# Edge convolution on one core: minimum trees two batches at a time over three tiles, and at most two chain steps in a row

## The chip, the cores and the metric

The kernel runs on one core of a Trainium2 chip. The core's engines work side by side and meet through semaphores: TensorE (PE in the profile, with its weight loads as PEld), VectorE (DVE), ScalarE (ACT), GpSimd (POOL) and SyncE (SP, which here only issues transfers). Each engine takes its instructions in the order in which the program holds them. The metric is the device time of one execution in microseconds (us), lower is better; the time of a kernel is the median of its runs.

## The reference

```python
def _L0_gnn_ref(x, W, b, edge_index):
    src, dst = (edge_index[0], edge_index[1])
    x_i = x[dst]
    x_j = x[src]
    feat = jnp.concatenate([x_i, x_j - x_i], axis=-1)
    msg = feat @ W.T + b
    out = jax.ops.segment_max(msg, dst, num_segments=x.shape[0])
    return jnp.where(jnp.isfinite(out), out, 0.0)
edge_index = jnp.stack([src, dst])
h = jnp.maximum(_layernorm(x, axis=-1), 0.0)
x = x + _L0_gnn_ref(h, L0_gnn_W, L0_gnn_b, edge_index)
```

There are 6250 nodes with 128 channels in float32 and 206250 edges (100000 random pairs in both directions, and a loop at every node), sorted by destination. The part of a message that belongs to the destination is the same for all its edges, so what has to be found is, for each destination and channel, the maximum over its sources j of one row `near[j]` = W2 h[j].

## The kernel before

Destinations lie on a grid of 128 partitions by 49 columns; sources are cut into 49 tiles of 128. After a first part (layer norm, products, and for each destination a sorted list of its sources) the maximum is taken in two ways at once.

**Dense part.** For each destination and each source tile t one edge, the winner, goes through TensorE. The minimum over |source - 256 t| along a destination's sorted list gives the winner's row in the tile. ScalarE makes these numbers (`distances(g)`, L616, one ACTIVATE for each of the two tiles of batch g), and VectorE takes the minimum by halving (`tree(g)`: L1326, L1331, then, once for each two batches, L1340 and L1345, which writes `M`). There are 25 batches. SP stores `M` to `winners` and loads it back broadcast over all partitions (784 KB for a tile, at most six tiles ahead); ScalarE turns it into a one-hot matrix (`one_hot(t)`, L621), and TensorE multiplies the tile's rows of `near` by it, in three bf16 parts, into PSUM: 39 matmuls of 481 columns for a tile, in four rounds of 12, 9, 9 and 9. After each round VectorE takes the maximum of PSUM and `acc` (`dense_round`, L1373). PSUM holds two rounds, so TensorE can start round n when VectorE is through with round n - 2.

**Chain.** Every edge that isn't a winner of its tile is a loser. Losers stand in a list of 504 steps (the last one is empty), a step holding one edge for each partition. For each step GpSimd gathers 128 rows of `near_table` (L765), four steps to a block; a block is issued when the block two before it has landed and when the chain has passed the slot that it overwrites, six blocks back. VectorE adds each step to a running maximum (`chain_step`, L1317). SP stores the running maxima eight steps at a time to `running_max` (L485), and a last gather, `finals` (L744, 49 of them, one for each column), takes for each destination the row at which its run ends. These finals overwrite the memory that the trees use, and the first of them waits until all trees are done. Nine groups of four are issued between gathers, after steps 432, 440, ... 496; the other 13 columns come behind the last gather, and the last two of these need the very last store. Then `join(g)` (L1430, L1432, 13 groups) takes the maximum of `acc` (transposed by TensorE) and these rows, adds the destination's own part, and SP stores the result in two or three transfers for each group (L517, L518, L521).

**What sets the order.** VectorE's program is one list of pieces, made by `schedule()`: the second list's sorting and compaction, then 49 tiles of four rounds, with tree pieces between them. Six trees stand ahead of the tiles (`EARLY_TREES`); before the change, one tree follows each of the tiles 0 to 18. The planner goes through the pieces with a cost for each and a model of the gathers, and puts up to `MOST_STEPS` chain steps behind a piece where their rows should have landed (`served`). Steps that find no place come after the tiles, mixed with the joins (`rest_steps`): 16 before the change. Of the other 488, all stand in runs of four: 25 runs ahead of the tiles, 97 in them. SP's order (stores, loads) follows the same list.

Of the kernel before, what the change touches and what calls it, by code (L numbers as in the profile page):

```python
# [45 lines left out]

CUTS = ((36, 400), (44, 472), (47, 496), (49, 504))
FINALS_FROM, FINALS_EVERY = 432, 8
LANDING, MARGIN, MOST_STEPS = 4.6, 1.5, 4
JOINS = 2  # L50
UNITS = ((0, 4), (4, 7), (7, 10), (10, 13))
PAD = 8190
# [9 lines left out]
def stages(h):  # L62
    a, z, _ = PARTS[h]
    return ((z - a) * KS + LEFT * h - 1).bit_length()


FLAG_PIECES, WORD_PIECES = 6, 5
EARLY_TREES = 6
TREES_FROM = 2


def window(g):

    per_tile, before, upto = 32.0 / 49, g // 2 * 4, min(g // 2 * 4 + 3, 48)
    low, high = per_tile * before, per_tile * upto
    first = max(0, math.floor(low - 2.75 * math.sqrt(low)))
    count = max(8, -(-(math.ceil(high + 2.75 * math.sqrt(high) + 2) - first) // 4) * 4)
    first = min(first, KM - count)
    return first, first + count


def last_halvings(g):

    first, end = window(g)
    n, left = (end - first) // 4, []
    while n > 2:
        n -= n // 2
        left.append(n)
    return left


def tree_pieces(g):

    first, end = window(g)
    half = (end - first) // 2 * 100
    costs = [0.17 + half * 0.00052, 0.17 + half * 0.00026]
    if g % 2 or g == 24:
        costs += [0.17 + n * 200 * 0.00052 for n in last_halvings(g)] + [0.4]
    return [("tree", c) for c in costs]


def schedule():

    pieces = [("lists", 11.0, 2.2), ("check", 1.1, 1.5), ("check", 1.9, 1.5), ("check", 1.9, 1.5)]
    pieces += [("sort", 1.42, 1.5)] * 21 + [("tiles", 2.3, 1.7)]
    pieces += [("flags", cost, 1.8) for cost in (2.05, 2.6, 2.5, 2.5, 1.4)]
    pieces += [("words", cost, 1.8) for cost in (3.5, 1.2, 1.2, 1.2, 3.0, 1.2, 3.0)]  # L110
    trees = 0
    for i in range(stages(1)):
        long = i < stages(1) - 3
        pieces += [("move", 1.5, 1.5)] + [("move", 0.8, 1.5)] * 4 if long else [("move", 0.8, 1.5), ("move", 1.3, 1.5)]
        if TREES_FROM <= i < TREES_FROM + EARLY_TREES:
            pieces += [(name, cost, 1.6) for name, cost in tree_pieces(trees)]
            trees += 1
    pieces += [("list", 2.2, 1.4), ("verdict", 0.2, 1.3)]
    pieces += [("disorder", 0.8, 1.3)]
    for t in range(49):  # L120
        for r in range(4):
            pieces += [("round", (2.15, 1.65, 1.65, 1.65)[r], 1.26)]
        if trees < 25:
            pieces += [(name, cost, 1.3) for name, cost in tree_pieces(trees)]
            trees += 1
    first, total = PARTS[0][2], PARTS[0][2] + PARTS[1][2]
    finals = {FINALS_FROM + g * FINALS_EVERY: GROUP for g in range(CUTS[0][0] // GROUP)}
    now, issue, n, landed, done, listed, steps = 0.0, 0.0, 0, [], [], None, []
    for name, cost, gather in pieces:
        now += cost  # L130
        if name == "list":
            listed = now
        here = []
        while n < total and len(here) < MOST_STEPS:
            if len(landed) <= n:
                b = n // GATHERS
                if n == first:
                    if listed is None:
                        break
                    issue = max(issue, listed)  # L140
                if b >= SLOTS:
                    issue = max(issue, done[(b - SLOTS + 1) * GATHERS - 1] + 0.2)
                if b >= FLYING:
                    issue = max(issue, landed[(b - FLYING) * GATHERS])
                issue += GATHERS * gather
                landed += [issue + LANDING] * GATHERS
                issue += 1.25 * finals.get((b + 1) * GATHERS, 0)
            if landed[n] + MARGIN > now:
                break
            now += 0.355  # L150
            done.append(now)
            here.append(n)
            n += 1
        steps.append(here)
    return [name for name, _, _ in pieces], steps, list(range(n, total)), first, total


def edgeconv(nc, x, src, dst, W, b, out):
# [10 lines left out]
    chk_p = 125  # L169
    chk_w = edges // chk_p  # L170
    CT = sum(c for _, _, c in PARTS)
    early_groups = CUTS[0][0] // GROUP
    spans = [(a, min(a + GROUP, tiles)) for a in range(0, tiles, GROUP)]
# [3 lines left out]
    batches = [(a, min(a + 2, tiles)) for a in range(0, tiles, 2)]  # L177
    rounds = len(UNITS)
    names, served, rest_steps, first_steps, all_steps = schedule()
    first_blocks, all_blocks = first_steps // STEPS, all_steps // STEPS  # L180
    assert D == P and tiles == 49 and rest and 0 < lastj and CUTS[-1] == (tiles, CT) and lastp == P - 1
# [15 lines left out]
    with ExitStack() as ctx:  # L197
# [337 lines left out]
        def _(act):  # L535
# [72 lines left out]
            def distances(g):  # L608
                if g == 0:
                    act.wait_ge(k2_ready, 2)  # L610
                if g >= 2:
                    act.wait_ge(y_free, g - 1)
                a, z = batches[g]
                first, end = window(g)
                for t in range(a, z):
                    nc.scalar.activation(y[g % 2][:, t - a, 0:end - first, :], k2[:, first:end, :], ACT.Abs,  # L616
                                         bias=off[:, t:t + 1]).then_inc(y_made, 1)

            def one_hot(t):
                act.wait_ge(bytes_in[t % OHS], 16 * (t // OHS + 1))  # L620
                nc.scalar.activation(oh[t % OHS], oh_bytes[t % OHS], ACT.Abs_reciprocal_sqrt, bias=spike[:, 0:1],  # L621
                                     scale=float(SPIKE), saturate=False).then_inc(oh_ready, 1)

            a, z, _ = PARTS[1]
            numbers, at = words[1][1], LEFT + (z - a) * KS
# [9 lines left out]

            for g in range(EARLY_TREES):
                distances(g)
            for t in range(tiles):
                one_hot(t)
                if t + EARLY_TREES < len(batches):  # L640
                    distances(t + EARLY_TREES)

        def edge_by_edge(pool):
            HALF = P // 2
# [65 lines left out]
        def _(pool):  # L710
# [24 lines left out]
            for h, (a, z, _) in enumerate(PARTS):  # L735
                pool.wait_ge(starts_ready, h + 1)
                for j in range(a + a % 2, z, 2):
                    nc.gpsimd.indirect_dma_start(L_pairs[:, j // 2, :], None, src_pad[:, None],  # L738
                                                 bass.IndirectOffsetOnAxis(start_i[:, j:j + 1], 0)).then_inc(list_in[h], 16)
# [43 lines left out]
            for (a, _), (z, cap) in zip(CUTS, CUTS[1:]):  # L783
                stored(cap // STEPS)
                finals(a, z)
# [670 lines left out]
```

## Time and profile before

| what | value |
|---|---|
| time, median of 3 runs | 839.28 us (838.05 to 840.8) |
| time of the profiled execution | 839.78 us |
| its span, first to last instruction | 838.1 us |
| mean granted TensorE clock | 0.881 of full speed |
| busy: VectorE, GpSimd, TensorE, ScalarE | 92%, 69%, 65%, 50% of the span |

The span is 1.7 us shorter than the time of the same execution, which holds some work around it. Busy shares are means over the whole span. GpSimd's gathers each show about 0.94 us of busy time and 0.3 us ahead of the next one, so an engine that issues gathers without a pause shows some 75% busy.

### The profile page before, as it was taken

To read this page: it belongs to the slowest core of one execution; us is meant where nothing else is said; L and a number is where in the kernel's file an instruction comes from. 1 tells how busy PE (TensorE), PEld (TensorE's weight loads), DVE (VectorE), ACT (ScalarE), POOL (GpSimd) and SP (SyncE) were. 2 spreads that over 40 slices of the span, in tenths; PEclk is the share of its full clock that TensorE was granted. 3 is DMA by queue.
4 is the path that set the end of the run, shared out by engine and by line. 5 is a ranking of instruction groups with operands and counts; after the bars stand their busy time and mean duration, and the time that the engine had idled before them with its cause. 6 is when DMAs were issued, how large, how long until landed. Compare 5 with 4: busy or idle time off the path is not lost.

```text
span 838.1 us, 7993 instructions
## 1 busy us (share of the span) xinstructions
PE 540.9 (65%) x2442; PEld 260.6 (31%) x2442; DVE 767.7 (92%) x1264; ACT 422.2 (50%) x279; POOL 579.0 (69%) x609
## 2 busy tenths in 40 slices
PE   1564898000006678676767667888888888888871
PEld 1553466000002233232322222333333333333340
DVE  8999999989997998899898999899999998888896
ACT  3876314520390756567565878555555556560000
POOL 1650477777777777677777777777777777777772
PEclk9999899555557998898988897999999999999995
DMA  8590023232647655555555555556555666642336
GB/s 251 148 254 26 16 69 98 69 101 79 201 101 226 173 174 144 167 167 155 176 146 163 153 180 155 177 186 193 180 178 173 187 179 181 218 129 77 103 101 197
DMA packets 114071, 126.77 MB, mean 151 GB/s; under 512 B 19176, under 2 KB 96470, under 8 KB 113885
## 3 DMA queue, kind: packets, MB, share of 16 engines
q1 hardware_dynamic: 95090, 86.33, 33.9%
q0 software_dynamic: 18752, 38.98, 17.7%
q10 hardware_dynamic: 186, 0.96, 0.3%
q8 instruction: 19, 0.31, 0.2%
q14 instruction: 24, 0.20, 0.1%
HBM read 86.46 MB, written 40.57 MB: 152 GB/s over the span
## 4 chain that ended last, share of the span: by engine, by line
DVE 35%; PE 18%; issue 15%; DVEq 0%
DVE acc L1373 20%; PE ps L888 18%; DVE maxima L1317 10%; DVE hT L1326 2%; DVE hT L1430 1%; DVE hT L1340 1%; DVE hT L1331 1%; DVEq L1372 0%; DVE M L1345 0%; DVE hT L1432 0%; PE ps L876 0%; DVEq L1313 0%; DVEq L913 0%; DVEq L1330 0%; DVE spare L1351 0%
## 5 line engine op out<-in xcount | busy, mean ns | idle before, releaser
L765 POOL DMA_INDIRECT rows<-near_table,idx x503 | 502.6, 999 | 202.1 <-issue 137.6
L1373 DVE TENSOR_TENSOR acc<-ps,acc 128x1924 f32<-128x1924 f32 x196 | 343.7, 1780 | 35.0 <-PE ps L888 34.6
L888 PE MATMUL ps<-ohs,near 128*128 128x481 fp8e3 x1404 | 320.4, 383 | 84.9 <-DVE acc L1373 76.6
L621 ACT ACTIVATE ohs<-ohs,spike 128x6272 fp8e3<-128x6272 uint8 x36 | 197.8, 5513 | 70.6 <-DMA ohs<-winners 70.6
L888 PEld LDWEIGHTS ps<-ohs,near 128*128 128x128 bf16 x1404 | 134.8, 101 | 270.5 <-DVE acc L1373 95.3
L1317 DVE SCALAR_TENSOR_TENSOR maxima<-maxima,fresh,rows 128x128 f32<-128x128 f32 x503 | 177.1, 352 | 13.6
L616 ACT ACTIVATE hT<-k,off 128x1600 bf16<-128x1600 int16 (+6 forms) x49 | 65.9, 1391 | 148.0 <-DVE hT L1331 148.0
L888 PE MATMUL ps<-sorts_mem,near 128*128 128x481 fp8e3 x507 | 114.9, 381 | 29.0 <-DVE acc L1373 26.9
L621 ACT ACTIVATE sorts_mem<-sorts_mem,spike 128x6272 fp8e3<-128x6272 uint8 x13 | 71.7, 5515 | 30.8 <-DMA sorts_mem<-winners 30.8
L888 PEld LDWEIGHTS ps<-sorts_mem,near 128*128 128x128 bf16 x507 | 48.8, 101 | 94.9 <-DVE acc L1373 31.7
L876 PE MATMUL ps<-flags,ones 128*128 128x14 f32 x2 | 0.6, 368 | 113.7 <-DVE spare L1351 113.7
L744 POOL DMA_INDIRECT hT<-running_max,end_row x49 | 47.4, 968 | 19.0 <-issue 14.0
L738 POOL DMA_INDIRECT ohs<-src_pad,start_i x25 | 25.0, 1000 | 19.3 <-DVE start_i L1002 12.3
L876 PEld LDWEIGHTS ps<-flags,ones 128*128 128x128 f32 x2 | 0.5, 310 | 113.9 <-issue 113.9
L1279 DVE COPY_PREDICATED ohs<-ohs 128x556 int32<-128x556 int32 (+9 forms) x40 | 29.7, 742 | 1.1
L603 ACT COPY base<-ps 128x512 f32<-128x512 f32 (+1 forms) x13 | 7.3, 561 | 40.7 <-PE ps L859 40.7
L859 PEld LDWEIGHTS ps<-wT,hT 128*128 128x128 f32 x98 | 23.5, 310 | 5.1 <-issue 3.7
L830 PE MATMUL ps<-wT,hT 128*128 128x128 f32 x98 | 13.9, 286 | 15.8 <-ACT near L588 15.8
L804 PE MATMUL ps<-ident,k 128*128 128x128 f32 x49 | 9.1, 311 | 22.6 <-ACT k L558 22.6
L859 PE MATMUL ps<-wT,hT 128*128 128x128 f32 x98 | 22.4, 373 | 0.0
L1326 DVE TENSOR_TENSOR hT<-hT 128x1600 bf16<-128x1600 bf16 (+7 forms) x25 | 20.6, 826 | 0.0
L558 ACT ACTIVATE k<-acc,shift,rstd 128x128 f32<-128x128 f32 x49 | 20.1, 482 | 0.6 <-DVE shift L983 0.6
(200 smaller groups left out, 425.3 us busy)
## 6 DMA issues: line engine op xcount, KB each, us to landing
running_max<-maxima SPq DMA_DIRECT2D x63, 512.0 KB, 3.6
ohs<-winners SPq DMA_DIRECT2D x36, 784.0 KB, 6.5
sorts_mem<-winners SPq DMA_DIRECT2D x13, 784.0 KB, 6.6
rows<-near_table,idx POOLq DMA_INDIRECT x503, 3.3
acc<-in_x SPq DMA_DIRECT2D x6, 512.0 KB, 6.1
near_table<-acc SPq DMA_DIRECT2D x12, 256.0 KB, 5.3
base<-in_x SPq DMA_DIRECT2D x1, 2744.0 KB
out_x<-hT SPq DMA_DIRECT2D x12, 224.0 KB
```

Source lines behind the costliest of these rows:

```text
L558: last = nc.scalar.activation(xn[:, g % 2, j - spans[g][0], :], x_nat[:, j, :], ACT.Identity, bias=shift[:, j:j + 1], scale=rstd[:, j:j + 1])
L616: nc.scalar.activation(y[g % 2][:, t - a, 0:end - first, :], k2[:, first:end, :], ACT.Abs, bias=off[:, t:t + 1]).then_inc(y_made, 1)
L621: nc.scalar.activation(oh[t % OHS], oh_bytes[t % OHS], ACT.Abs_reciprocal_sqrt, bias=spike[:, 0:1], scale=float(SPIKE), saturate=False).th ...
L738: nc.gpsimd.indirect_dma_start(L_pairs[:, j // 2, :], None, src_pad[:, None], bass.IndirectOffsetOnAxis(start_i[:, j:j + 1], 0)).then_inc( ...
L744: nc.gpsimd.indirect_dma_start(rowsF[:, j, :], None, running_max[0:cap * P, :], bass.IndirectOffsetOnAxis(end_row[:, j:j + 1], 0)).then_in ...
L765: nc.gpsimd.indirect_dma_start(rows[:, n % (SLOTS * GATHERS), :], None, near_table[:, :], bass.IndirectOffsetOnAxis(idx[:, n:n + 1], 0)).t ...
L859: last = nc.tensor.matmul(bank(g % 3)[:, (j - a) * D:(j - a + 1) * D], hT[:, j:j + (P - 1) * tiles + 1:tiles], wT[:, 1, :], start=False, s ...
L888: last = nc.tensor.matmul(bank(4 * (n % 2) + c - UNITS[r][0])[:, 0:CHUNK], near[:, t, part, :], oh[t % OHS][:, at:at + CHUNK], start=part ...
L1279: then(V.copy_predicated(word[:, u:v], moves[:, u:v], word[:, u + d:v + d]))
L1317: V.scalar_tensor_tensor(run_at(n + 1), run_at(n), fresh[:, n:n + 1], rows[:, n % (SLOTS * GATHERS), :], ALU.add, ALU.max).then_inc(chain, 1)
L1326: then(V.tensor_tensor(mine[:, 0:n, 0:half, :], mine[:, 0:n, 0:half, :], mine[:, 0:n, half:2 * half, :], ALU.min))
L1373: V.tensor_tensor(into, found[:, 0:z - a, 0:CHUNK], into, ALU.max).then_inc(max_done, 1)
```

## The change

The trees of two batches (four tiles) are now one group of pieces, spread over the twelve rounds of three tiles; the ten groups stand in tiles 2 to 31. ScalarE's distances for such a group come in one go, after the one-hot matrix of the tile before it. A run of chain steps has at most two steps. The planner's costs for rounds and steps are a little lower. The computation is the same. The number of trees, rounds, steps, gathers and transfers is the same.

```diff
-LANDING, MARGIN, MOST_STEPS = 4.6, 1.5, 4
+LANDING, MARGIN, MOST_STEPS = 4.6, 1.5, 2
+STEP, NEXT_STEP = 0.26, 0.38
...
+TREE_TILES, TREES_AT = 3, 2
...
+def pair_begins(k):
+    return TREES_AT + TREE_TILES * (k - EARLY_TREES // 2)
+
+
+def pair_pieces(k):
+    return [piece for g in range(2 * k, min(2 * k + 2, 25)) for piece in tree_pieces(g)]
...
-            pieces += [("round", (2.15, 1.65, 1.65, 1.65)[r], 1.26)]
-        if trees < 25:
-            pieces += [(name, cost, 1.3) for name, cost in tree_pieces(trees)]
-            trees += 1
+            pieces += [("round", (2.1, 1.6, 1.6, 1.6)[r], 1.26)]
+            k = (t - TREES_AT) // TREE_TILES + EARLY_TREES // 2
+            if t >= TREES_AT and k <= 12:
+                at, late = (t - pair_begins(k)) * 4 + r, pair_pieces(k)
+                pieces += [(name, cost, 1.3) for name, cost in late[at * len(late) // (4 * TREE_TILES):
+                                                                    (at + 1) * len(late) // (4 * TREE_TILES)]]
...
-            now += 0.355
+            now += NEXT_STEP if here else STEP
...
-                if t + EARLY_TREES < len(batches):
-                    distances(t + EARLY_TREES)
+                for k in range(EARLY_TREES // 2, -(-len(batches) // 2)):
+                    if t == pair_begins(k) - 1:
+                        for g in range(2 * k, min(2 * k + 2, len(batches))):
+                            distances(g)
```

On VectorE, tile 9 stood before as follows (`acc<-ps` is a round, `maxima` the chain steps, `hT` and `M` the tree):

```order
L1373 TENSOR_TENSOR acc<-ps,acc 128x1924
L1373 TENSOR_TENSOR acc<-ps,acc 128x1443
L1317 SCALAR_TENSOR_TENSOR maxima<-maxima,fresh,rows 128x128 x4
L1373 TENSOR_TENSOR acc<-ps,acc 128x1443 x2
L1317 SCALAR_TENSOR_TENSOR maxima<-maxima,fresh,rows 128x128 x4
L1326 TENSOR_TENSOR hT<-hT 128x2x800
L1331 TENSOR_TENSOR hT<-hT 128x2x400
L1340 TENSOR_TENSOR hT<-hT 128x4x200
L1340 TENSOR_TENSOR hT<-hT 128x4x100
L1317 SCALAR_TENSOR_TENSOR maxima<-maxima,fresh,rows 128x128 x4
L1345 SCALAR_TENSOR_TENSOR M<-hT 128x200
```

In the changed kernel, whose line numbers are 12 to 14 higher, tile 9 holds:

```order
L1387 TENSOR_TENSOR acc<-ps,acc 128x1924
L1387 TENSOR_TENSOR acc<-ps,acc 128x1443
L1331 SCALAR_TENSOR_TENSOR maxima<-maxima,fresh,rows 128x128 x2
L1340 TENSOR_TENSOR hT<-hT 128x2x700
L1331 SCALAR_TENSOR_TENSOR maxima<-maxima,fresh,rows 128x128 x2
L1387 TENSOR_TENSOR acc<-ps,acc 128x1443
L1331 SCALAR_TENSOR_TENSOR maxima<-maxima,fresh,rows 128x128 x2
L1345 TENSOR_TENSOR hT<-hT 128x2x350
L1331 SCALAR_TENSOR_TENSOR maxima<-maxima,fresh,rows 128x128 x2
L1387 TENSOR_TENSOR acc<-ps,acc 128x1443
```

The tree's pieces stand singly, with two steps on either side; before, thirteen instructions stood between the last round of this tile and the first of the next. The steps come to 96 in 48 runs ahead of the tiles, 376 in 188 runs in them, and 32 behind them.

Behind the last round, VectorE's program ended before with 15 steps and 13 joins (two rows each), which began:

```order
L1317 SCALAR_TENSOR_TENSOR maxima<-maxima,fresh,rows 128x128 x8
L1430 TENSOR_TENSOR hT<-ps,hT 128x512
L1432 TENSOR_TENSOR hT<-hT,base 128x512
L1430 TENSOR_TENSOR hT<-ps,hT 128x512
L1432 TENSOR_TENSOR hT<-hT,base 128x512
L1317 SCALAR_TENSOR_TENSOR maxima<-maxima,fresh,rows 128x128 x4
```

Nine joins then stood behind the last step. Now 31 steps follow the tiles, two joins after each four of them, and the program ends so (the first row is the last run of steps):

```order
L1331 SCALAR_TENSOR_TENSOR maxima<-maxima,fresh,rows 128x128 x7
L1444 TENSOR_TENSOR hT<-ps,hT 128x512
L1446 TENSOR_TENSOR hT<-hT,base 128x512
L1444 TENSOR_TENSOR hT<-ps,hT 128x512
L1446 TENSOR_TENSOR hT<-hT,base 128x512
L1444 TENSOR_TENSOR hT<-ps,hT 128x512
L1446 TENSOR_TENSOR hT<-hT,base 128x512
L1444 TENSOR_TENSOR hT<-ps,hT 128x128
L1446 TENSOR_TENSOR hT<-hT,base 128x128
```

Nine joins moved ahead of the last step, and four are left behind it. On SP the stores of eight groups' results moved ahead of the last store of running maxima, and five are left behind it. GpSimd's order is unchanged.

## Rows read from the trace of the kernel before

**Rows 1.** Timeline of GpSimd: start, us, instruction, [idle before it, and its releaser].
```profile
94.17 1.25 POOL L765 DMA_INDIRECT rows<-near_table,idx  x1 [38.16 <-DVE idx L1300]
...
805.01 0.94 POOL L765 DMA_INDIRECT rows<-near_table,idx  x1 [0.30 <-issue]
...
819.54 1.03 POOL L744 DMA_INDIRECT hT<-running_max,end_row  x1 [0.30 <-issue]
824.99 0.94 POOL L744 DMA_INDIRECT hT<-running_max,end_row  x1 [4.41 <-DMA running_max<-maxima]
826.23 0.94 POOL L744 DMA_INDIRECT hT<-running_max,end_row  x1 [0.31 <-issue]
```

**Rows 2.** Waits of the whole span, GpSimd's gathers: us in total, times, longest.
```profile
POOL rows L765 <- issue: 137.6, 443, 1.4
...
POOL rows L765 <- DMA rows<-near_table,idx: 17.1, 34, 3.4
...
POOL rows L765 <- DVE maxima L1317: 9.3, 25, 1.3
```

**Rows 3.** Waits of the whole span, VectorE's rounds and ScalarE's distances.
```profile
ACT hT L616 <- DVE hT L1331: 148.0, 21, 31.6
...
DVE acc L1373 <- PE ps L888: 34.6, 47, 3.9
```

**Rows 4.** Issue to landing of transfers from 780 us on, count, us.
```profile
hT<-running_max,end_row POOLq DMA_INDIRECT x19, 2.6
rows<-near_table,idx POOLq DMA_INDIRECT x15, 2.5
```

**Rows 5.** Timeline of VectorE behind the last round (809.88 us on).
```profile
809.88 3.12 DVE L1317 SCALAR_TENSOR_TENSOR maxima<-maxima,fresh,rows 128x128 f32<-128x128 f32 x8
812.92 0.68 DVE L1430 TENSOR_TENSOR hT<-ps,hT 128x512 f32<-128x512 f32 x1
...
820.71 0.68 DVE L1430 TENSOR_TENSOR hT<-ps,hT 128x512 f32<-128x512 f32 x1
...
831.32 0.28 DVE L1430 TENSOR_TENSOR hT<-ps,hT 128x128 f32<-128x128 f32 x1
831.64 0.29 DVE L1432 TENSOR_TENSOR hT<-hT,base 128x128 f32<-128x128 f32 x1
```

**Rows 6.** Timeline of SP's issues behind the last chain step.
```profile
820.82 0.36 SPq L485 DMA_DIRECT2D running_max<-maxima  x1
821.22 0.58 SPq L517 DMA_DIRECT2D out_x<-hT  x1
...
835.36 0.38 SPq L517 DMA_DIRECT2D out_x<-hT  x1
835.79 0.45 SPq L518 DMA_DIRECT2D out_x<-hT  x1
```

**Rows 7.** Timeline of VectorE in tiles without trees (638 to 653 us).
```profile
638.62 3.72 DVE L1373 TENSOR_TENSOR acc<-ps,acc 128x1924 f32<-128x1924 f32 x2
642.26 1.51 DVE L1317 SCALAR_TENSOR_TENSOR maxima<-maxima,fresh,rows 128x128 f32<-128x128 f32 x4
643.68 3.23 DVE L1373 TENSOR_TENSOR acc<-ps,acc 128x1443 f32<-128x1443 f32 x2
646.82 1.51 DVE L1317 SCALAR_TENSOR_TENSOR maxima<-maxima,fresh,rows 128x128 f32<-128x128 f32 x4
```

**Rows 8.** Timeline of VectorE, the last step of a run of four and what follows.
```profile
419.78 0.35 DVE L1317 SCALAR_TENSOR_TENSOR maxima<-maxima,fresh,rows 128x128 f32<-128x128 f32 x1
420.05 0.36 DVE L1345 SCALAR_TENSOR_TENSOR M<-hT 128x200 uint8<-128x200 bf16 x1
```

**Rows 9.** Busy us (and instructions) by engine in two stretches, granted clock, DMA share, GB/s.
```profile
420.40:515.70 95.30, 67.67 (x273) 27.67 (x273) 87.47 (x131) 69.82 (x20) 72.05 (x74) 0.86 0.58 161
...
613.00:700.00 87.00, 74.88 (x350) 32.72 (x351) 82.85 (x101) 48.30 (x10) 64.84 (x70) 1.00 0.64 197
```

**Rows 10.** Pieces of the chain that ended last, start, us: rounds on TensorE.
```profile
693.57 2.64 PE ps L888 x12
...
710.50 2.03 PE ps L888 x9
```

**Rows 11.** Costliest groups, ScalarE's one-hot matrices and distances: busy us, mean ns.
```profile
L621 ACT ACTIVATE ohs<-ohs,spike 128x6272 fp8e3<-128x6272 uint8 x36 | 197.8, 5513 | 70.6 <-DMA ohs<-winners 70.6
...
L616 ACT ACTIVATE hT<-k,off 128x1600 bf16<-128x1600 int16 (+6 forms) x49 | 65.9, 1391 | 148.0 <-DVE hT L1331 148.0
```

## The prediction, made before the changed kernel ran

> **What bounds the kernel now.** VectorE is busy for 92% of the span, so the eye goes there first. The stage that ends last says something else. I read GpSimd's timeline, then its waits, then the tail on VectorE and SP, and only then the rounds.
>
> GpSimd issues its first gather at 94.17 and its last one, step 502, at 805.01 [rows 1]. In these 710.8 us it issues 503 gathers and 32 of the finals. Each shows 0.94 us and 0.30 us ahead of the next, 1.25 us in all [rows 1], so 535 of them need at least 669 us. Its waits beyond that 0.30 are few: on landings 17.1 - 34 x 0.30 = 6.9 us, on the chain's slots 9.3 - 25 x 0.30 = 1.8 us, and under "issue" 137.6 - 443 x 0.30 = 4.7 us [rows 2]; the rest up to 711 us are gathers that take longer than 0.94 us, most of them ahead of the tiles. So GpSimd runs from 94 us to the end with 13.4 us of waiting in it. It is a second bound beside VectorE, and the change gives it no instruction less.
>
> VectorE ends its rounds at 809.88 [rows 5], 5 us behind the last gather's issue, still with 15 steps to do. Behind that the tail of before has a chain of its own. The last step leaves at 820.71 [rows 5]. SP stores the maxima at 820.82 [rows 6], and GpSimd, through with 11 finals at 819.54 + 1.03 = 820.57, waits 4.41 us for that store and issues the last two finals at 824.99 and 826.23 [rows 1]. Nine joins stand behind the last step, the last at 831.32 [rows 5], and SP issues all 13 results behind the last store, until 835.79 + 0.45 = 836.24 [rows 6]; the span ends 1.9 us later. SP's row of issues ends last here.
>
> **What the change does on VectorE.** Number of operations: equal. What it saves is the space between chain steps. A run of four takes 643.68 - 642.26 = 1.42 us until the next instruction [rows 7]; the last step of a run hands over after 420.05 - 419.78 = 0.27 us [rows 8], so a step that the next step waits for costs (1.42 - 0.27)/3 = 0.38 us. A run of two then costs 0.38 + 0.27 = 0.65 us, an estimate, since none stands in the trace. Ahead of the tiles: 25 x 1.42 = 35.5 before, 48 x 0.65 = 31.2 now, 4.3 less. In the tiles: 97 x 1.42 = 137.7 before, 188 x 0.65 = 122.2 now, 15.5 less. So with nothing else the rounds end at 809.9 - 19.8 = 790.1.
>
> Here the Trainium skill speaks against the change: "VectorE: DVE Perf Modes", section "The DRAIN you can't avoid", says that the next instruction doesn't start until the pipeline is empty and that chaining operations without semaphores doesn't avoid it, so what counts is the number of operations. By that, 503 steps would cost the same in any order and the 19.8 us would be nothing. This trace doesn't agree: 0.27 us against 0.38 us for the same operation [rows 7, 8].
>
> The second saving is VectorE's wait for TensorE, 34.6 us in 47 waits [rows 3]. One kind comes where three rounds stand in a row. The other follows thirteen instructions in a row between two rounds: TensorE fills its two halves of PSUM and idles, its granted clock falls from 2.4 to 1.2 GHz for a part of the time (0.86 of full speed as a mean over 420 to 516 us with trees, 1.00 over 613 to 700 without, [rows 9]), and its next rounds are late. With tree pieces singly between rounds both should shrink. Bounds: nothing is saved, 790; all is saved, 755. All isn't likely: in tiles 32 to 48 the rounds cost VectorE 3.64 + 3.14 = 6.78 us [rows 7] and 49 runs of two in 17 tiles 1.9 us, 8.7 in all, and TensorE needs 2.64 + 3 x 2.03 = 8.7 us for the same tile [rows 10], so each will wait for the other a little. I take half: **the rounds end near 772**.
>
> The trees' own operations are the same and are as long as before. Finals wait for the last tree, now in tile 31; tile 31 ends 17 tiles of 8.7 us ahead of 772, near 624, and the first final comes behind gather 431, which is 71 gathers and 32 finals of 1.25 us ahead of 805, near 676. So this wait costs nothing; if tile 31 ended behind 676, each us of it would delay GpSimd.
>
> **What it does to the end.** VectorE at 772 is ahead of GpSimd's last gather by 33 us. So the 31 steps and nine joins that follow the rounds go at the pace of the gathers. They need 31 x 0.38 + 9 x 1.33 = 23.8 us (a join: (831.32 - 820.71)/8 = 1.33 us, [rows 5]). The last step then comes right behind the landing of the last gather, 805.0 + 2.5 [rows 4] + three steps = 808.7, and its store is done 4.2 us later (820.82 to 824.99 [rows 1, 6]), at 813. GpSimd is only then in the middle of its 11 finals, which end at 820.57 as before. It issues the last two without a wait at 820.9 and 822.1, 4.1 us sooner than before. They land 2.6 us later [rows 4], at 823.5 and 824.7. Joins 9 and 10 are done by then; join 11 takes 1.33 us to 824.8, join 12 0.61 us (831.32 to 831.64 + 0.29, [rows 5]) to 825.5. SP has issued all other results; the two left take 0.43 us for each of four transfers [rows 6], until 826.7, and end 1.9 us later: **828.6**, if the last gather goes out at 805.0 as before. Of the 9.5 us, 4.1 are the wait ahead of the last finals; the rest is SP's queue of results and the joins, which now lie ahead of the last step.
>
> The last gather's time is the other term. VectorE is earlier, so the waits on slots (1.8 us) should go; I count the waits on landings as they are. That gives 803.2 and a span of 826.8. Bounds for it: all 13.4 us of waits go, 791.6, end 815; the waits on landings double, since 49 loads of 784 KB now come within a shorter time, 6.9 us more, end 835.5.
>
> The profiled execution's time lies 1.7 us above its span, so 826.8 is 828.5; the median of the runs lies 0.5 us below that execution, which gives **828**.
>
> **Where the gain stops being tied to VectorE.** The last store has to be done by 820.6, so the last step by 816.4, so the rounds by 816.4 - 23.8 = 792.6. Below that, an earlier end of the rounds is worth nothing; above, each us of theirs is one of the end's, and the end is theirs + 36. I expect 772, and the case in which no wait is saved, 790, still lies below. By the page's rule on chained operations that case would be 810 and the middle one 792: the forecast would hold only with half of the waits gone.
>
> **Rivals.**
> *VectorE stays the pace, and the kernel is slower.* Place: ScalarE. Distances now come as four ACTIVATEs in a row, 4 x 1.39 = 5.6 us, between one-hot matrices of 5.5 us [rows 11], ten times, and the second half waits for memory that the group before frees late in its second tile. ScalarE already waits 148.0 us for that memory, 21 times [rows 3]. If the one-hot matrix behind a group is late by x, TensorE and VectorE lose 10 x. Against it: by the new order the memory is free some 1.3 tiles (14 us at 10.7 us a tile) ahead of the tile that needs the matrix, ScalarE then needs 2.8 + 5.5 = 8.3 us, and TensorE wants it about 0.3 tile early, which leaves about 2.5 us. It decides from x = 2.1 us (rounds at 793); the kernel is slower by over 0.3% from rounds at 805, x = 3.3 us. At x = 4: rounds at 812, end 848, time about 849.
> *The gathers get slower* by more transfers in the way: 7 us more of waiting, end 835.5, time 837, within or just beyond 0.3%. For it: loads come closer together in tiles 0 to 31. Against: behind 772 there are none at all, and the DMA share is at 0.57 to 0.64 in both kinds of tile [rows 9] without many waits.
> *The gathers get faster*: an end of 815 to 821, time 816 to 822. For it: slots are freed earlier and the trees' stores are spread. Against: only 13.4 us are there to be had.
> *No change*: if the tail were bound by the number of steps left behind the rounds (16 more, 6 us) the gain would be eaten. That holds only with rounds beyond 793, the first rival's case.
>
> **How the numbers follow.** Forecast (gathers set the end, time 823 to 832): 0.68. Gathers faster, 815 to 823: 0.09. Gathers slower, 832 to 842: 0.12, more than half of it still faster by 0.3%. VectorE late: 0.11, of which 0.07 above 842. What a measurement can tell from no change is about 0.3%, 2.5 us: 836.8 to 841.8. So faster 0.84, same 0.09, slower 0.07. The range 820 to 838 leaves out the fastest end and VectorE late, somewhat under 0.2.
>
> **What would show it.** Right: GpSimd's gathers at the same pace with the last one at 800 to 806; no wait of GpSimd ahead of the last two finals; the rounds over between 755 and 790, and VectorE idle on gathers behind them; runs of two at 0.65 us; TensorE's clock in the tree tiles above 0.9; SP's last result issued within 3 us of the last join. Wrong: the last round beyond 793, ScalarE's one-hot matrices as releaser of TensorE, or gathers whose waits on landings have grown by more than 5 us.

## The result, and the profile after

| | before | after |
|---|---|---|
| time, median (range) of 20 runs each | 840.19 us (838.05 to 842.98) | 835.38 us (825.92 to 839.66) |
| time of the profiled execution | 839.78 us | 828.43 us |
| its span | 838.1 us | 826.8 us |
| granted TensorE clock | 0.881 | 0.892 |

The ratio of after to before is 0.9921, with a 95% interval of 0.9897 to 0.9946: faster by 0.8%, where the prediction said 1.3%. The runs of after spread over 14 us, those of before over 5. The profiled execution is the slowest of five runs of after that lie apart (825.92 to 828.43 us; the other 15 start at 833.3), 7 us below the median; that has to be kept in mind with every number of its trace.

Busy time by engine, from the page of after (us, share of the span, instructions):

```profile
PE 527.7 (64%) x2442; PEld 254.9 (31%) x2442; DVE 749.0 (91%) x1264; ACT 421.4 (51%) x279; POOL 579.7 (70%) x609
```

The timeline of VectorE in after, around the end of the rounds and in the tail, answers to [rows 5] and [rows 7] (start, us, instruction, [idle before it, and its releaser]):

```profile
754.04 0.73 DVE L1331 SCALAR_TENSOR_TENSOR maxima<-maxima,fresh,rows 128x128 f32<-128x128 f32 x2
754.69 1.65 DVE L1387 TENSOR_TENSOR acc<-ps,acc 128x1443 f32<-128x1443 f32 x1
...
759.12 1.66 DVE L1387 TENSOR_TENSOR acc<-ps,acc 128x1443 f32<-128x1443 f32 x1
760.69 3.58 DVE L1331 SCALAR_TENSOR_TENSOR maxima<-maxima,fresh,rows 128x128 f32<-128x128 f32 x9
...
784.07 1.51 DVE L1331 SCALAR_TENSOR_TENSOR maxima<-maxima,fresh,rows 128x128 f32<-128x128 f32 x4 [6.40 <-DMA rows<-near_table,idx]
...
803.28 1.12 DVE L1331 SCALAR_TENSOR_TENSOR maxima<-maxima,fresh,rows 128x128 f32<-128x128 f32 x3 [0.93 <-DMA rows<-near_table,idx]
...
820.21 0.29 DVE L1446 TENSOR_TENSOR hT<-hT,base 128x128 f32<-128x128 f32 x1
```

The rounds end at 759.12 + 1.66 = 760.8, 49 us sooner than in [rows 5]. A run of two takes 754.69 - 754.04 = 0.65 us. From there VectorE has time to spare: it stands still for rows, up to 6.40 us at once, and its last step is done at 803.28 + 1.12 = 804.4. So in these two traces 49 us were gained on VectorE and 11 us at the end of the span.

The timeline of GpSimd in after, beside [rows 1]:

```profile
800.70 0.94 POOL L779 DMA_INDIRECT rows<-near_table,idx  x1 [0.30 <-issue]
...
815.79 0.94 POOL L758 DMA_INDIRECT hT<-running_max,end_row  x1 [0.30 <-issue]
817.04 0.94 POOL L758 DMA_INDIRECT hT<-running_max,end_row  x1 [0.30 <-issue]
```

The last gather is issued at 800.70 (before: 805.01), and the last two finals come without the 4.41 us of waiting that [rows 1] showed. Here is the end of SP's timeline, beside [rows 6], and then the closing instructions of GpSimd and SP, put down to L209, where the program's context is opened and closed (durations in ns: least, median, most; then the start in us; the record of GpSimd's begins while it still issues finals):

```profile
821.26 0.46 SPq L530 DMA_DIRECT2D out_x<-hT  x1
```

```profile
L209 POOLq DRAIN  x1: 18653/18653/18653, 807.9 to 807.9; - x1
...
L209 SPq DRAIN  x1: 7/7/7, 822.9 to 822.9; - x1
```

SP is through at 822.9. The span goes on to 826.8, and what ends then is GpSimd's closing instruction: 807.9 + 18.65 = 826.55. That is 8.6 us behind the end of its last final, 817.04 + 0.94. In before the same instruction (its L197) was hidden:

```profile
L197 POOLq DRAIN  x1: 10989/10989/10989, 824.8 to 824.8; - x1
```

It ends at 824.8 + 10.99 = 835.8, again 8.6 us behind the last final (826.23 + 0.94), and 0.4 us ahead of SP's last issue (836.24, [rows 6]). So in after GpSimd ends last, with its gathers, its finals and 8.6 us behind them, of which 826.55 - 822.9 = 3.7 us lie beyond SP's end.

Waits of the whole span in after, beside [rows 2] and [rows 3] (us in total, times, longest):

```profile
ACT hT L628 <- DVE hT L1345: 148.9, 21, 31.7
...
POOL rows L779 <- issue: 134.7, 440, 0.6
...
DVE acc L1387 <- PE ps L902: 17.0, 22, 3.9
DVE hT L1444 <- DMA hT<-running_max,end_row: 16.7, 4, 5.4
DVE maxima L1331 <- DMA rows<-near_table,idx: 12.9, 5, 6.4
...
POOL rows L779 <- DMA rows<-near_table,idx: 11.7, 36, 1.0
...
POOL rows L779 <- DVE maxima L1331: 11.4, 25, 2.9
...
PEld ps L902 <- ACT ohs L633: 3.2, 3, 1.6
```

VectorE waits for TensorE half as long as before, 17.0 us for 34.6. GpSimd's waits beyond 0.30 us for each gather are (134.7 - 132.0) + (11.7 - 10.8) + (11.4 - 7.5) = 7.5 us in this execution, 13.4 before.

### The profile page after: what moved, and what is told of

It is laid out like the page before. It is cut to its first block, busy times and chain, and to the rows that moved or that the text cites. A ratio compares the mean times of both kernels' runs of the same rounds, so it can differ in the third digit from the quotient of the medians.

```text
span 826.8 us, 7994 instructions
## 1 busy us (share of the span) xinstructions
PE 527.7 (64%) x2442; PEld 254.9 (31%) x2442; DVE 749.0 (91%) x1264; ACT 421.4 (51%) x279; POOL 579.7 (70%) x609
## 4 chain that ended last, share of the span: by engine, by line
DVE 29%; issue 22%; PE 13%; POOL 4%; DMA 1%; POOLq 0%; DVEq 0%
DVE acc L1387 20%; PE ps L902 13%; DVE maxima L1331 7%; POOL rows L779 2%; POOL hT L758 2%; DMA rows<-near_table,idx 1%; DVE hT L1340 1%; DVE hT L1345 0%; DVE hT L1354 0%; DMA hT<-running_max,end_row 0%; DVE M L1359 0%; POOLq L209 0%; DVE hT L1444 0%; DVEq L1386 0%; DVE hT L1446 0%
## 5 line engine op out<-in xcount | busy, mean ns | idle before, releaser
L779 POOL DMA_INDIRECT rows<-near_table,idx x503 | 503.4, 1001 | 196.3 <-issue 134.7
L902 PE MATMUL ps<-ohs,near 128*128 128x481 fp8e3 x1404 | 306.2, 367 | 64.5 <-DVE acc L1387 62.2
L902 PEld LDWEIGHTS ps<-ohs,near 128*128 128x128 bf16 x1404 | 128.5, 97 | 242.3 <-DVE acc L1387 69.8
L1331 DVE SCALAR_TENSOR_TENSOR maxima<-maxima,fresh,rows 128x128 f32<-128x128 f32 x503 | 175.2, 348 | 23.3 <-DMA rows<-near_table,idx 12.9
L902 PE MATMUL ps<-sorts_mem,near 128*128 128x481 fp8e3 x507 | 114.1, 377 | 21.7 <-DVE acc L1387 20.8
L633 ACT ACTIVATE sorts_mem<-sorts_mem,spike 128x6272 fp8e3<-128x6272 uint8 x13 | 71.3, 5511 | 13.8 <-DMA sorts_mem<-winners 13.7
L758 POOL DMA_INDIRECT hT<-running_max,end_row x49 | 47.0, 959 | 14.9 <-issue 13.7
L1444 DVE TENSOR_TENSOR hT<-ps,hT 128x512 f32<-128x512 f32 (+1 forms) x13 | 8.5, 654 | 16.7 <-DMA hT<-running_max,end_row 16.7
L1340 DVE TENSOR_TENSOR hT<-hT 128x1600 bf16<-128x1600 bf16 (+7 forms) x25 | 20.8, 831 | 0.0
```

The source lines that it names most:

```text
L758: nc.gpsimd.indirect_dma_start(rowsF[:, j, :], None, running_max[0:cap * P, :], bass.IndirectOffsetOnAxis(end_row[:, j:j + 1], 0)).then_in ...
L779: nc.gpsimd.indirect_dma_start(rows[:, n % (SLOTS * GATHERS), :], None, near_table[:, :], bass.IndirectOffsetOnAxis(idx[:, n:n + 1], 0)).t ...
L902: last = nc.tensor.matmul(bank(4 * (n % 2) + c - UNITS[r][0])[:, 0:CHUNK], near[:, t, part, :], oh[t % OHS][:, at:at + CHUNK], start=part ...
L1331: V.scalar_tensor_tensor(run_at(n + 1), run_at(n), fresh[:, n:n + 1], rows[:, n % (SLOTS * GATHERS), :], ALU.add, ALU.max).then_inc(chain, 1)
L1340: then(V.tensor_tensor(mine[:, 0:n, 0:half, :], mine[:, 0:n, 0:half, :], mine[:, 0:n, half:2 * half, :], ALU.min))
```

## The experiments

My theory after this: GpSimd's row of gathers and finals sets the end as soon as the rounds end ahead of about 793. Behind the row come 8.6 us that outlast every other engine, and the medians lie above the profiled execution because the row waits more in most executions. The first rival: VectorE's time still counts, and the gain of 0.8% is what is left of its 49 us. The second: the tail (steps, joins, SP) sets the end. Each kernel below was timed with runs of before on the same chip; before had a median of 840.05 us (17 runs) beside the parts alone, the single fills and the eight gathers, and of 841.04 us (17 runs) beside the other four.

### Runs of two alone

Made in before:

```diff
-LANDING, MARGIN, MOST_STEPS = 4.6, 1.5, 4
+LANDING, MARGIN, MOST_STEPS = 4.6, 1.5, 2
+STEP, NEXT_STEP = 0.26, 0.38
...
-            pieces += [("round", (2.15, 1.65, 1.65, 1.65)[r], 1.26)]
+            pieces += [("round", (2.1, 1.6, 1.6, 1.6)[r], 1.26)]
...
-            now += 0.355
+            now += NEXT_STEP if here else STEP
```

> Runs of at most two chain steps, with the planner's new costs, but one tree after each of the tiles 0 to 18 as before (32 steps behind the rounds). Theory A (GpSimd's row of gathers sets the end as soon as VectorE's rounds end before about 793 us): the shorter runs alone save some 20 us of VectorE, the rounds end between 780 and 790, and the kernel is nearly as fast as the whole change, ratio to before 0.988 to 0.995. Theory B (the spread trees bring the gain, by TensorE's clock and VectorE's waits): ratio 0.998 to 1.002.

Measured: 833.21 us (831.12 to 834.46, 6 runs), ratio 0.9912 (0.9894 to 0.993). The last round, the last gather and the last final, from its timelines, and VectorE's wait for TensorE:

```profile
776.37 1.66 DVE L1374 TENSOR_TENSOR acc<-ps,acc 128x1443 f32<-128x1443 f32 x1
```

```profile
806.20 0.94 POOL L766 DMA_INDIRECT rows<-near_table,idx  x1 [0.30 <-issue]
...
822.86 0.94 POOL L745 DMA_INDIRECT hT<-running_max,end_row  x1 [0.30 <-issue]
```

```profile
DVE acc L1374 <- PE ps L889: 28.5, 38, 4.1
```

The rounds end at 776.37 + 1.66 = 778.0, 32 us ahead of before (2 more than expected) and 17 behind after, and the time is that of after. The shorter runs alone, with the 16 steps that they move behind the tiles, carry the whole gain. They do so at a granted clock of 0.874 over the span, no higher than the 0.881 of before.

### Spread trees alone

Made in after:

```diff
-LANDING, MARGIN, MOST_STEPS = 4.6, 1.5, 2
-STEP, NEXT_STEP = 0.26, 0.38
+LANDING, MARGIN, MOST_STEPS = 4.6, 1.5, 4
+STEP, NEXT_STEP = 0.355, 0.355
...
-            pieces += [("round", (2.1, 1.6, 1.6, 1.6)[r], 1.26)]
+            pieces += [("round", (2.15, 1.65, 1.65, 1.65)[r], 1.26)]
```

> Trees of two batches over three tiles, but runs of up to four chain steps with the planner's old costs (16 steps behind the rounds as before). Theory A: the waits of VectorE for TensorE shrink by about half, 17 us, the rounds end near 793, the last gather goes out near 801, GpSimd is then the last to end; ratio 0.988 to 0.996. Theory B': the short runs bring the gain, and trees alone save nothing: ratio 0.998 to 1.002, rounds at 805 to 810.

Measured: 833.56 us (832.76 to 834.76, 6 runs), ratio 0.9923 (0.9908 to 0.9938).

```profile
793.68 1.65 DVE L1387 TENSOR_TENSOR acc<-ps,acc 128x1443 f32<-128x1443 f32 x1
```

```profile
804.64 0.94 POOL L779 DMA_INDIRECT rows<-near_table,idx  x1 [0.30 <-issue]
...
821.55 0.95 POOL L758 DMA_INDIRECT hT<-running_max,end_row  x1 [0.30 <-issue]
```

The rounds end at 795.3, 2.7 us behind the predicted threshold of 792.6, and the last final still goes out without a wait. But that threshold isn't this kernel's. Its tail is that of before: 15 steps and four joins stand ahead of the last store instead of 31 and nine, and they took 820.71 - 809.88 = 10.8 us in [rows 5] instead of the 23.8 that the prediction put. By the prediction's own sum the point then lies at 816.4 - 10.8 = 805.6. This part alone carries the whole gain too. The two gains don't add up: each takes the rounds out of the way, and the second finds nothing left to take. That speaks against the first rival, by which 778, 795 and 761 would give three different times. It speaks against the second as well: nine joins and their results stand behind the last step here, four in after and in runs of two alone, and the three end alike.

### A little more work for VectorE

One fill of 128 columns behind each of the last 116 rounds (`EXTRA_FROM, EXTRA = 20, 128`); nothing reads it.

Made in after, in `dense_round`:

```diff
+                if n >= EXTRA_FROM * rounds:
+                    settled()
+                    then(V.memset(ones[:, 0:EXTRA], 1.0))
```

> The changed kernel with one more VectorE instruction, a fill of 128 columns that nobody reads, behind each round from tile 20 on (116 of them, some 0.15 us each, 17 us in all). Theory A: the rounds end near 778 instead of 760.8, and the end doesn't move: ratio to before as the changed kernel, 0.990 to 0.995. Rival (VectorE still sets the pace): 17 us more, ratio 1.010 to 1.015.

Measured: 833.68 us (829.85 to 835.81, 6 runs), ratio 0.9913 (0.989 to 0.9935): no cost. But the dose was weak. In its timeline a fill shows 0.17 us and the next round begins 0.08 us behind its start:

```profile
702.51 0.17 DVE L1391 MEMSET ones<- 128x128 f32 x1
702.59 1.60 DVE L1388 TENSOR_TENSOR acc<-ps,acc 128x1443 f32<-128x1443 f32 x1
```

The rounds end at 763.32 + 1.65 = 765.0, 4.2 us later than in after, where 17 were expected; in the second trace of after (below), without any fill, they end at 765.3. So it isn't shown that the fills moved them at all, and with 32 us free this run shows little; the next one was made for that.

### Much more work for VectorE

Four such fills, each behind the one before it, after each of the last 100 rounds.

Made in after, the constants at the top and the rest in `dense_round`:

```diff
+EXTRA_FROM, EXTRA = 24, 4
...
+                if n >= EXTRA_FROM * rounds:
+                    for _ in range(EXTRA):
+                        settled()
+                        then(V.memset(ones[:, :], 1.0))
```

> The changed kernel with four fills of 128 columns, each waiting for the one before, behind each round from tile 24 on (100 rounds, 0.6 to 0.7 us each, 60 to 70 us in all, of which some 12 go into waits that are there anyway). Theory A, with VectorE late: the rounds end at 810 to 820, beyond 793, so the tail of 31 steps and nine joins, 24 us, then 4.2 us of store, two finals and GpSimd's 8.6 us at its end come behind them: end 850 to 862, ratio 1.013 to 1.027. Rival (the end never hangs on the rounds here): ratio 0.990 to 0.995.

Measured: 879.2 us (878.47 to 880.3, 4 runs), ratio 1.0462 (1.0441 to 1.0482). From its timelines and its waits:

```profile
642.69 0.94 DVE L1392 MEMSET ones<- 128x128 f32 x4
643.55 0.68 DVE L1332 SCALAR_TENSOR_TENSOR maxima<-maxima,fresh,rows 128x128 f32<-128x128 f32 x2
...
829.78 1.65 DVE L1388 TENSOR_TENSOR acc<-ps,acc 128x1443 f32<-128x1443 f32 x1
```

```profile
851.32 1.02 POOL L780 DMA_INDIRECT rows<-near_table,idx  x1 [0.30 <-issue]
...
868.33 0.94 POOL L759 DMA_INDIRECT hT<-running_max,end_row  x1 [0.30 <-issue]
```

```profile
POOL rows L780 <- DVE maxima L1332: 62.5, 47, 4.3
```

The rounds end at 831.4, beyond the threshold, and now VectorE's time counts: the direction is as the theory has it. The size and the path are not. A round's four fills cost 643.55 - 642.69 = 0.86 us, 86 us for 100 rounds, of which 70.6 show in the end of the rounds. And the end comes 878.1 - 831.4 = 46.7 us behind the rounds, not 36: the chain is so late that GpSimd waits for its slots, 62.5 - 47 x 0.30 = 48 us in all, and the last gather itself moves to 851.3. The last final waits for nothing but its place in the row (0.30 us), and the end comes 878.1 - 851.3 = 26.8 us behind the last gather, 26.1 in after. So it is the last gather that made this run late, through the slots, and not the last store, by which the prediction worked out its 793. My "end = rounds + 36" held the last gather fixed. Slots tie GpSimd to VectorE once VectorE is far behind.

### Eight more gathers

Behind each of eight blocks between block 60 and 88, one more gather into memory of its own, which nothing reads but SP's wait at the end.

Made in after (the memory `more`, the semaphore `more_in` and SP's wait for it are left out here):

```diff
+MORE = list(range(60, 92, 4))
...
+                if b in MORE:
+                    k = MORE.index(b)
+                    nc.gpsimd.indirect_dma_start(more[:, k, :], None, near_table[:, :],
+                                                 bass.IndirectOffsetOnAxis(idx[:, 4 * b:4 * b + 1], 0)).then_inc(more_in, 16)
```

> The changed kernel with eight more gathers on GpSimd, into memory that nobody reads, one behind each fourth block from step 240 on. Theory A: each costs a place of 1.25 us in the row that sets the end, 10 us in all: ratio to before 1.001 to 1.007, the last gather of the chain near 811. Rival (VectorE sets the pace): no change against the changed kernel, ratio 0.990 to 0.995.

Measured: 842.5 us (837.69 to 846.3, 12 runs), ratio 1.0029 (1.0012 to 1.0046). That is 0.95 to 1.1% above the two measurements of after (0.9934, below, and 0.9921), 8 to 9 us for 8 x 1.25 = 10 us of GpSimd. Its last final, beside 817.04 of after, and its waits:

```profile
826.30 0.94 POOL L762 DMA_INDIRECT hT<-running_max,end_row  x1 [0.30 <-issue]
```

```profile
POOL rows L783 <- issue: 136.2, 445, 0.6
...
POOL rows L783 <- DVE maxima L1339: 11.8, 26, 2.0
POOL rows L783 <- DMA rows<-near_table,idx: 10.0, 31, 0.9
```

9.3 us later. The profiled execution is the fastest of the 12 here, but its waits beyond 0.30 us, (136.2 - 133.5) + (11.8 - 7.8) + (10.0 - 9.3) = 7.4 us, are those of the first trace of after (7.5), so the two can be compared. The rounds end at 766.28 + 1.66 = 767.9, far out of the way. So 10 us given to GpSimd cost 8 to 9, and the weak dose given to VectorE cost nothing.

### Three blocks in flight, in after

Made in after:

```diff
-FLYING = 2
+FLYING = 3
```

> The changed kernel, with three blocks of gathers in flight instead of two: a block is issued when the block three before it has landed. Theory A: GpSimd sets the end and its waits on landings beyond the usual 0.30 us (5 to 11 us a run) go, so the last gather goes out near 796 and the end comes 4 to 10 us sooner than the changed kernel's: ratio to before 0.980 to 0.987, with less spread from run to run. Rival (the waits move to the slots, or gathers get slower when more are in flight): ratio 0.990 to 0.995, as the changed kernel.

Measured: 824.08 us (823.54 to 825.05, 5 runs), ratio 0.9809 (0.9792 to 0.9825), the fastest of all. Its waits and the ends of its rows:

```profile
POOL rows L779 <- issue: 136.8, 449, 0.3
...
POOL rows L779 <- DVE maxima L1331: 8.5, 28, 0.3
POOL rows L779 <- DMA rows<-near_table,idx: 7.6, 25, 0.3
```

```profile
796.18 0.94 POOL L779 DMA_INDIRECT rows<-near_table,idx  x1 [0.30 <-issue]
...
812.66 0.94 POOL L758 DMA_INDIRECT hT<-running_max,end_row  x1 [0.30 <-issue]
```

None of these waits is longer than 0.3 us, and the 5 runs lie within 1.5 us, where 6 runs of after on the same chip lie within 6.6. The order of the program, the slots and VectorE's work are those of after. The waits that were put down to the chain (2.9 us the longest in after) went as well, so they were waits for landings: of two semaphores that a block waits for, the view had named the chain's. The trace of after bears this out. Here are the longest such wait and the steps of which the second frees that gather's slot:

```profile
566.42 0.94 POOL L779 DMA_INDIRECT rows<-near_table,idx  x1 [2.86 <-DVE maxima L1331]
```

```profile
552.01 0.73 DVE L1331 SCALAR_TENSOR_TENSOR maxima<-maxima,fresh,rows 128x128 f32<-128x128 f32 x2
```

The slot was free at 552.74, 13.7 us before the gather went out. In both traces of after, every gather into a used slot that stood more than 0.32 us idle went out at least 3.1 us after its slot was free.

### The same in before

The edit is the same, made in before.

> The kernel before, with three blocks in flight. Theory A: here VectorE's rounds end at 810 whatever GpSimd does, so an earlier last gather is worth nothing: ratio 0.997 to 1.002. Rival (GpSimd alone set the end of the kernel before, too): ratio 0.985 to 0.993.

Measured: 839.87 us (838.94 to 841.01, 12 runs), ratio 0.9993 (0.9983 to 1.0003): nothing.

```profile
801.53 0.94 POOL L765 DMA_INDIRECT rows<-near_table,idx  x1 [0.30 <-issue]
...
823.65 0.95 POOL L744 DMA_INDIRECT hT<-running_max,end_row  x1 [4.19 <-DMA running_max<-maxima]
```

The last gather goes out 3.5 us sooner (801.53 for 805.01), and the last two finals wait 4.19 us for the store as ever. In before the rounds (808.9 here) and the tail behind them set the end; with the rounds gone the gathers do. The same edit is worth nothing in one and more than the change itself in the other.

### After once more

No edit: a second profile of after, since the first profiled execution lay 7 us below the median.

> The changed kernel once more, for a second trace beside these. Ratio 0.990 to 0.995. If its span is above 830, the theory says that the last gather is later by the same amount, by longer waits on landings, and that the rounds end below 770 again.

Measured: 835.1 us (831.85 to 838.4, 6 runs), ratio 0.9934 (0.991 to 0.9957), profiled at 835.88 us.

```profile
763.66 1.66 DVE L1387 TENSOR_TENSOR acc<-ps,acc 128x1443 f32<-128x1443 f32 x1
```

```profile
807.83 0.96 POOL L779 DMA_INDIRECT rows<-near_table,idx  x1 [0.30 <-issue]
...
824.49 0.95 POOL L758 DMA_INDIRECT hT<-running_max,end_row  x1 [0.31 <-issue]
```

```profile
POOL rows L779 <- issue: 131.7, 429, 0.7
POOL rows L779 <- DVE maxima L1331: 18.7, 37, 1.8
POOL rows L779 <- DMA rows<-near_table,idx: 13.8, 36, 2.2
```

Beyond 0.30 us each, the waits are (131.7 - 128.7) + (18.7 - 11.1) + (13.8 - 10.8) = 13.6 us, 6.1 more than in the first profile, and the last gather comes 7.1 us later. The rounds end at 763.66 + 1.66 = 765.3. So the 7 us between the two executions of after are for the most part GpSimd's waits.

## Why the prediction was right, and where its sizes were off

**Right.** GpSimd was the second bound, and the end is tied to it as soon as the rounds end early enough. Shown by kernels with rounds at 761, 778 and 795 that end alike, by the eight gathers, and by the two runs with three blocks in flight. The plainest sign is the distance from the last gather to the end of the span: 26.1 to 26.8 us in all eight traces of after, its parts and its variants, with the rounds over anywhere from 760 to 831; 33.1 and 36.1 us in the two kernels with the rounds of before. The threshold near 793 isn't shown: with the tail that it was worked out for, rounds at 778 cost nothing and rounds at 831 cost by another path, the slots. The wait ahead of the last two finals went, as worked out; the last step came 804.4 - 800.7 = 3.7 us behind the last gather, as worked out.

**The rounds: 760.8, taken as 772.** Within the bounds of 755 to 790. Half of the wait for TensorE went, as chosen (17.0 of 34.6 us left), and the granted clock in the tiles with trees rose from 0.86 ([rows 9]) to 0.99, the 2.4 GHz level for nearly the whole stretch:

```profile
400.00:516.00 116.00, 90.14 (x408) 37.60 (x407) 112.42 (x160) 82.97 (x26) 88.01 (x91) 0.99 0.60 178
```

But steps and waits, as summed, make only 19.8 + 17.6 = 37.4 of the 49.2 us. The rest is in terms that the prediction put at nothing. Counted from the start of each instruction to the start of the next, waits left out, the steps ahead of the rounds' end take 175.7 us before and 153.7 after (22.0 less, not 19.8); the tree pieces in the tiles 39.85 and 34.87 (5.0 less), since a small piece (L1340 of before) takes 0.48 us where a piece that needs it follows, and 0.28 us where a step does; the sorting and other work ahead of the tiles 209.4 and 206.3 (3.1 less); the rounds 336.2 and 333.5 (2.7 less). Other waits grew by 1.2 us. With the 17.6 that makes 49.2. It changes nothing at the end.

The case for the order of steps was decided by the trace. With runs of two alone the rounds end 31.9 us sooner, of which 34.6 - 28.5 = 6.1 us are waits for TensorE and 20.8 us are steps (175.7 to 154.9 us, counted as above): a step hands over after 0.27 us to an instruction that doesn't need its result and after 0.38 us to one that does. Even a bare count of operations would have given something, since 18 of the 488 steps moved behind the last round: 18 x 0.36 = 6.5 us. The prediction had set the Trainium skill against this, "VectorE: DVE Perf Modes", section "The DRAIN you can't avoid". It left out a sentence of the same paragraph there, "A next op that is not held starts earlier". So the section doesn't speak against the change, and the trace agrees with that sentence of the Trainium skill: a step shows 0.35 us of its own, and the instruction that doesn't need it starts 0.27 us behind its start [rows 8].

**The end behind the last final: a term left out.** I let the span end with SP's last result, 6.5 us behind the last final (828.6 - 822.1). It ends 826.8 - 817.0 = 9.75 us behind it, because GpSimd's closing instruction takes until 8.6 us after its last final. That is 3.3 us more than the sum had. The trace of before held it (it ended 0.4 us ahead of SP's last issue), and the prediction left it out, since SP's row ended last there.

**The last gather: a term of the right kind with the wrong size.** Forecast 803.2; 800.7 in the first profile, 807.8 in the second. I counted the waits on landings as they were in one execution. They are not the same in each: 7.5 us and 13.6 us of waiting for the same kernel, where the sum had 13.4 - 1.8 = 11.6. In before this hardly shows, since there GpSimd's time isn't the last. Waits aren't all of it. The second profile waits no longer than before did, and its last gather still goes out 2.8 us later than the 805.0 of before. The gathers themselves took 2.4 us longer (502.6 us busy in before, 505.0 in the second profile):

```profile
L765 POOL DMA_INDIRECT rows<-near_table,idx x503 | 502.6, 999 | 202.1 <-issue 137.6 <-DVE idx L1300 38.2 <-DMA rows<-near_table,idx 17.1
```

```profile
L779 POOL DMA_INDIRECT rows<-near_table,idx x503 | 505.0, 1004 | 202.3 <-issue 131.7 <-DVE idx L1314 38.2 <-DVE maxima L1331 18.7
```

The first profiled execution met the predicted span of 826.8 to the tenth, by two errors that cancel: the last gather 2.5 us sooner and the last final another 0.8 us sooner than worked out, and 3.3 us more behind it; that is luck. The median, 7 us above that execution, is the fairer judge: 835.4 for 828, inside the range of 820 to 838, but in the interval that the prediction gave to slower gathers (832 to 842, chance 0.12) and not in that of its forecast (823 to 832, chance 0.68). The second profile, 0.5 us from the median, shows where the 7.4 us between its span and the predicted one lie: the last gather 807.8 - 803.2 = 4.6 us later, the last final 0.4 us sooner behind it than worked out, and 3.2 us more behind that.

**Rivals.** ScalarE's one-hot matrices held TensorE's weight loads up for 3.2 us in three places (2.0 in two before), and the rounds ended early: that rival is out. "The gathers get slower" gave 837 and lies nearest to the median. That waits for landings decide the last gather was right. That the change makes them longer wasn't shown, since the kernels with two blocks in flight and the rounds ending at 761 to 795 have 7 to 14 us of waits, and before had 13.4.

**Sums of the prediction.** Nine groups of finals, 36 and not 32, stand between the first gather and the last: 539 places of 1.25 us are 674 us, not 669, and the first final comes near 671, not 676. Neither changes the forecast. The 10.7 us a tile in the first rival stands in no row; in after the 49 tiles take 504.0 / 49 = 10.3 us each.

**Open.** Why the landings, and the gathers themselves, take longer in one execution than in another, what GpSimd does in the 8.6 us, and where VectorE's time begins to count with the tail of after.

## What to carry to other kernels

A second engine with only 13 us of waiting in its row caps what the first can gain; work out that cap, and where the cap lies in the distribution of runs, before adding up the savings, for two savings that each reach it are worth one. Once the bound has moved, retry the edits that did nothing before: one more block in flight gave 0.9993 in before and took the ratio from 0.993 to 0.981 in after. And when the last engine changes, look up what that engine still does behind its last useful instruction; another engine's tail may have hidden it.

## What the runs showed of the hardware that was not expected

- GpSimd's closing instruction ends 8.57 to 8.58 us behind the end of its last indirect transfer's instruction, in all ten traces of before, after and the experiments, with the time of the end anywhere from 822 to 878 us. It costs nothing while another engine ends later (before), and as much as it outlasts the others when GpSimd ends last (3.7 us beyond SP in after).
- With two blocks of four gathers in flight, GpSimd's waits differed by 6.1 us between two executions of after (7.5 and 13.6 us); with three, in the one trace of it, none is over 0.3 us, and the runs lie within 1.5 us instead of 6.6.
- A VectorE fill of 128 columns behind a round shows 0.17 us, and the next instruction begins 0.08 us behind its start; four in a row, each behind the other, take 0.86 us. Extra work must be measured from start to start when it serves as a dose.
